# Receiver half of a graph layer's first product: a table of values per node, read through masked hidden values of 128 consecutive edges

## What is computed

```python
r = edge_vec / norm(edge_vec);  sh1 = sqrt(3) * r
xs, xd = x[edge_src], x[edge_dst]
s1 = concat([xs[:, :8], xd[:, :8]])                 # 16 scalars
v1 = concat([xs[:, 8:], xd[:, 8:]]).reshape(E,16,3) # 16 vectors
w  = mlp(emb, fc1_w1, fc1_w2)                       # hidden 16 -> 512 weights per edge
s_t = a1 * (s1 @ Wss + vdot1 @ Wvv)                 # per edge 16 -> 8
v_t = a1 * ((s1 @ Wsv) * sh1 + v1 @ Wvs)
w2 = mlp(emb, fc2_w1, fc2_w2)                       # 384 weights per edge
scal, gates, vecs = second product of s_t, v_t, w2
edge_out = [tanh(scal), vecs * tanh(gates)] * norm
x = layernorm(x + segment_sum(edge_out, edge_dst))
```

## Time and profile before

| | |
|---|---|
| median of 3 runs | 6061.76 us |
| profiled execution, first to last instruction (span) | 6434.2 us |
| PE / DVE busy in it | 5895.3 / 5884.2 us (92% / 91%) |
| POOL / ACT busy in it | 4974.7 / 3993.5 us (77% / 62%) |
| DMA engines, mean busy share | about 0.43 in the loop |
| granted PE clock, mean | 0.983 of 2.4 GHz |

### The profile page before, as it was taken

One profiled execution on the slowest core, in us unless ns is written; L12 is line 12 of the kernel. 1 busy time (PEld: TensorE's weight loads), 2 busy tenths in 40 slices (PEclk: granted clock), 3 DMA queues, 4 the chain that ended last, 5 costly groups with the idle time before them and its releaser, 6 DMA issues. The chain is left out here.

```text
span 6434.2 us, 221220 instructions
## 1 busy us (share of the span) xinstructions
PE 5895.3 (92%) x68616; PEld 5688.0 (88%) x68616; DVE 5884.2 (91%) x7326; ACT 3993.5 (62%) x12507; POOL 4974.7 (77%) x6875
## 2 busy tenths in 40 slices
PE   4999999999999999999999999999999999999997
PEld 3898989889999988988999889889989899999997
DVE  7899999999999998989999989999999899999998
ACT  5666666666666666666666666666666566666663
POOL 6777777777778777877877778777878778787884
PEclk9999999999999999999999999999999999999998
DMA  5444444444444444444444444444444444444442
GB/s 144 89 87 85 88 91 87 86 88 89 87 88 91 86 88 88 89 86 85 92 87 87 87 85 91 86 86 88 92 86 92 85 86 93 86 93 87 92 88 54
DMA packets 1671119, 569.93 MB, mean 89 GB/s; under 512 B 1535146, under 2 KB 1619083, under 8 KB 1670536
## 3 DMA queue, kind: packets, MB, share of 16 engines
q1 hardware_dynamic: 1567911, 516.43, 36.8%
q0 software_dynamic: 103168, 53.03, 6.0%
HBM read 302.19 MB, written 7.26 MB: 48 GB/s over the span
## 5 line engine op out<-in xcount | busy, mean ns | idle before, releaser
L1043 PE MATMUL p<-identity,prods 128*128 128x128 f32 x29016 | 3580.0, 276 | 157.1 <-issue 81.0
L654 POOL DMA_INDIRECT nodes<-x_rows,idx x3224 | 3104.0, 963 | 704.7 <-issue 615.1
L1043 PEld LDWEIGHTS p<-identity,prods 128*128 128x128 f32 x29016 | 3219.4, 143 | 185.0 <-issue 163.6
L1038 PE MATMUL pw<-w_stack,hid_t 128*128 128x128 bf16 x22568 | 1679.3, 220 | 229.6 <-issue 110.8
L1038 PEld LDWEIGHTS pw<-w_stack,hid_t 128*128 128x128 bf16 x22568 | 1435.3, 99 | 316.6 <-issue 138.9
L1292 DVE TENSOR_TENSOR prods<-pw,V 128x2048 f32<-128x2048 f32 x403 | 922.6, 2289 | 177.2 <-remote 83.3
L1337 DVE TENSOR_TENSOR prods<-pw,M 128x1024 f32<-128x1024 f32 x806 | 975.9, 1211 | 15.9 <-issue 6.7
L1347 DVE TENSOR_TENSOR prods<-pw,VT 128x1536 f32<-128x1536 f32 x403 | 704.8, 1749 | 59.7 <-remote 53.2
L870 ACT ACTIVATE off_hot<-node_iota,off_base 128x42 f32<-128x42 f32 x3216 | 747.1, 318 | 0.0
L1314 DVE TENSOR_TENSOR prods<-pw,S 128x1024 f32<-128x1024 f32 x403 | 490.0, 1216 | 84.6 <-PE pw L1038 76.0
L610 POOL TENSOR_TENSOR vr<-V,r 128x384 f32<-128x384 f32 x403 | 347.5, 862 | 244.9 <-issue 185.5
(11 more groups left out here) (136 smaller groups left out, 8242.5 us busy)
## 6 DMA issues: line engine op xcount, KB each, us to landing
dstb<-in_dst SPq DMA_DIRECT2D x403, 504.0 KB
nodes<-x_rows,idx POOLq DMA_INDIRECT x3224
emb_stack<-emb_parts SPq DMA_DIRECT2D x2418, 20.0 KB
emb<-in_emb_t SPq DMA_DIRECT2D x403, 40.0 KB
hid_t<-hid_parts SPq DMA_TRANSPOSE x806
idx<-in_src SPq DMA_DIRECT2D x403, 4.0 KB
xw<-x SPq DMA_DIRECT2D x403, 7.9 KB
vecs<-in_vec SPq DMA_DIRECT2D x403, 12.0 KB
```

The source lines that it names most:

```text
L654: nc.gpsimd.indirect_dma_start(nodes[:, p, t, side, :], None, x_rows, bass.IndirectOffsetOnAxis(ap=idx[:, p, side, t:t + 1], axis=0)).then ...
L1038: mm = nc.tensor.matmul(pw[:, slot, t, :], hid_t[:, layer, a.par, t, :], w2_stack[:, lo:lo + W], start=True, stop=True)
L1043: return nc.tensor.matmul(out, column, identity[:, :], start=first, stop=last, is_transpose=True)
```

## The change

For the receivers the product is turned around. For one node and one hidden unit h, the receiver's features times the part of `fc1_w2` that belongs to h is the same for all edges into that node. So a table is made: per node 16 rows (one per h) of 64 values. The value of an edge is the sum over h of its hidden value times the node's row h.

- `nodes_made` (PE, 2 matmuls of 256 columns, each period) and `nodes_out` (ACT) make 64 nodes of the table in two periods; `store_nodes` (SP, every second period) stores them to `t_rows` in DRAM and loads the features for the next 64. The first 4 groups of 64 are made in the setup.
- `load_near` (SP): for each of the 8 tiles of a block, a register load of the tile's first receiver, then a DMA of 128 rows of 64 f32 values (8 nodes by 16 h) from `t_rows`.
- `hidden_near` (PE, 2 matmuls of 512 columns) makes the hidden values of the first layer transposed, 8 times, one for each of 8 nodes; rows with a large negative bias (`off_rows_of`, loaded by `stack_off`) make the copies of the wrong nodes zero after the ReLU in `near_hidden` (ACT).
- `receivers` (PE): 8 f32 matmuls, K = 128, 64 columns, from masked hidden values and table rows, into PSUM bank `pz`. `node_scalars`, `receiver_dots` and accumulation in `pz` bring the result into the sums.
- The first layer's per-edge weights shrink from 512 to 256 columns (7 fills become 5) and DVE's first-layer products and their transposes to half. `off_rows`, `hot_rows`, `dst_rows_made`, `directions`, the loads of `dstb`, `xw`, `vecs`, inverse lengths and weights in the loop go. `out_sums_back` and `vectors_back` (ACT) go, and DVE's `vectors_made` comes.
- The edges of a tile are now 128 in a row. Receivers, senders, weights and unit vectors of all edges are transposed on PE in the setup, in 7 chunks of 4 x 128 tiles, and kept in SBUF (`r_all`, `w_all`) or stored as `rec`, `base_rows` and `off_rows_of`.
- The flag's conditions change: a tile may span at most 8 nodes, a block 42.

```diff
-L1, L2 = 512, 384
+L1, L2 = 256, 384
-KINDS = 7
+KINDS = 5
...
+            def load_near(a):
+
+                p = a.par
+                sp.wait_ge(near_base_in[p], a.k(16))
+                sp.sem_inc(begun, 1)
+                wait(sp, d_mm, a.before(2).n(1, 1))
+                sp.sem_inc(begun, 1)
+                wait(sp, t_stored, a.before(1).k(16, 16 * (LEAD - 1)))
+                sp.sem_inc(begun, 1)
+                for t in range(G):
+                    first = nc.sync.value_load(near_base[0:1, p, t:t + 1], min_val=0, max_val=N - 1)
+                    sp.dma_start(t_near[:, p, t, :], t_rows[bass.ds(first * H, NEAR * H), :]).then_inc(t_near_in[p], 16)
+
+            def store_nodes(a):
+
+                sp.wait_ge(t_out, a.n(1, 1 + 2 * LEAD))
+                sp.sem_inc(begun, 1)
+                sp.dma_start(t_nodes[bass.ds((a.half + LEAD) * CHUNK, CHUNK), :],
+                             t_stage[0:CHUNK, :, :, :, :].rearrange("n h a j w -> n (h a j w)")).then_inc(t_stored, 16)
+                sp.wait_ge(t_mm, a.n(1, 1 + 2 * LEAD))
+                sp.sem_inc(begun, 1)
+                sp.dma_start(xt[:, 0, :, :], x6[:, :, bass.ds((a.half + (LEAD + 1)) * CHUNK, CHUNK)]).then_inc(xt_in[0], 16)
...
+            def hidden_near(a, half):
...
+                nc.tensor.matmul(near_ps, w1_near[:, :, :].rearrange("k n h -> k (n h)"),
+                                 emb_stack[:, p, 512 * half:512 * half + 512], start=True, stop=True).then_inc(near_mm, 1)
...
+            def receivers(a, before, is_general):
...
+                for t in range(G):
...
+                        mm = nc.tensor.matmul(z[:, :, t, :], hid_near[:, P * t:P * t + P],
+                                              t_near[:, a.par, t, :].rearrange("p (c w) -> p c w", w=C), start=(t == 0), stop=(t == G - 1))
+                mm.then_inc(d_mm, 1)
...
-            def dst_rows_made(a):
...
-            def off_rows(a):
...
-            def hot_rows(a):
```

More of the change, by code:

```diff
@@ L9 @@
 WINDOW = 42
-ROWS = 3 * WINDOW
+NEAR = 8
 C = 8
@@ L1159, in body @@
                     if three is not None:
-                        scalar_sums_turned(three, None if five is None else five.n(windows, windows + more))
+                        scalar_sums_turned(three)
                     if four is not None:
                         out_sums(four)
+                    if two is not None:
+                        receivers(two, three, is_general)
                     if zero is not None:
                         hidden(zero, is_general)
-                    if two is not None:
-                        pe.wait_ge(pv_done, two.n(2, 2))
-                        fill(two, 2, at.par)
@@ L1168, in body @@
-                    if one is not None and not is_general:
-                        dst_rows_made(one)
                     if four is not None:
                         four_sums_turned(four, windows, more)
+                    if three is not None:
+                        if two is not None:
+                            pe.wait_ge(pss_done, two.n(1, 1))
+                        else:
+                            pe.wait_ge(pgf_done, three.n())
+                        fill(three, 2, at.par)
@@ L1180, in body @@
                         else:
[L1181 to L1185 removed]
                             pe.wait_ge(po_done, three.n(2))
[L1187 removed]
+                        fill(three, 3, at.par)
                     if two is not None:
                         scalar_sums(two)
+                    if one is not None and fast:
+                        hidden_near(one, 1)
@@ new lines, in _ @@
+            last = recs[:, NS - 1 - (NCH - 1) * BLOCKS * P // G, G:2 * G].bitcast(F32)
+            wait_kept(dve, NCH - 1, 1)
+            if NS != FULL:
+                done(nc.vector.scalar_tensor_tensor(last, last, 1.0, fresh[:, :], ALU.subtract, ALU.mult))
+                nc.vector.tensor_scalar(last, last, 1.0, None, ALU.add).then_inc(fresh_done, 1)
+            else:
+                nc.vector.sem_inc(fresh_done, 1)
+            first, period, most, least = (bounds[:, k, :] for k in range(4))
@@ new lines, in _ @@
+            over, other = excess[:, 0, :], excess[:, 1, :]
+            done(nc.vector.tensor_tensor(over, first, period, ALU.subtract))
+            done(nc.vector.tensor_tensor(other, over, most, ALU.add))
+            done(nc.vector.tensor_scalar(other, other, 1.0 - WINDOW, None, ALU.add))
+            done(nc.vector.scalar_tensor_tensor(over, over, -1.0, other, ALU.mult, ALU.max))
+            done(nc.vector.scalar_tensor_tensor(over, most, 1.0 - NEAR, over, ALU.add, ALU.max))
+            done(nc.vector.scalar_tensor_tensor(over, least, -1.0, over, ALU.mult, ALU.max))
```

1442 lines of the change are left out of this document (877 added, 565 removed).

## The result

| | before | after |
|---|---|---|
| median, us | 6061.61 (6059.76 to 6062.57) | **9650.29** (9647.01 to 9653.0) |
| ratio | | 1.5917 (95%: 1.5894 to 1.594) |
| span of a clean profiled execution, us | 6065.0 | 9650.3 |
| period of the loop, us | 14.68 | 23.17 |
| PE / DVE busy | 95% / 97% | 64% / 49% |

The kernel is 59% slower. All comparisons from here on are with that one.

What follows compares the result with a forecast made beforehand. SP's DMA-issuing queue was taken as the bound: 14.5 - 3.4 + 12.3 = 23.4 us a period. 240 + 403 x 23.4 + 45 = 9715 us under the profiler, times 0.942, gave 9150 us, range 7700 to 9900.

Steps and rivals of the forecast that it cites:

- SP's queue is the bound, and the change puts eight loads on it: SP's DMA-issuing queue, over 90% full before, goes from 14.5 to 23.4 us a period, far above PE's 12.8.
- 1.23 us a tile: Table load on SP's queue: register load 0.451, bounds check, register operation, DMA 0.331, gaps; eight times makes 9.85 us.
- The other items: SP's queue per period: near_base 0.47, stack_off 0.88, store_nodes 0.66, semaphores 0.44 us added; 3.4 us of old loads gone.
- Eight f32 products, 1.2 to 3.1 us: PE's eight f32 matmuls of `receivers` with 64 columns: between 1.2 and 3.1 us a period, taken as 1.6.
- Setup 240 and tail 45: Outside the loop: 240 us until the loop's first product (84 before, range 160 to 300), and 45 us after it.
- times 0.942: Factor on the whole sum, median 6061.76 over profiled span 6434.2 us, turning 9715 us under the profiler into 9150.
- Without the profiler a period takes 14.7, which is the 14.6 of DVE and PE work: Kernel before, loop: the unprofiled period of 14.7 us equals the 14.6 us that DVE and PE work.
- DVE 11.4, PE 12.8 us a period: Compute work in the changed loop: DVE falls from 14.6 to 11.4 us, PE to 12.8 us (12.4 to 14.3).
- Busy under 60% for PE: Sign expected in the profile after: PE busy under 60% and DVE under 50%, idle time mostly ended by DMAs.
- The queue hides its issues: Rival on SP's queue: durations mostly the profiler's, or loads overlap DMAs; PE-bound at 5570 us, chance 0.12.
- The gaps alone are the profiler's: Rival on SP's queue: 80 gaps of 0.045 us vanish, 19.8 us a period, 7790 us; included in the 0.80.
- PE at its lower clock becomes the bound: Rival on PE: at 1.2 GHz its work doubles at most to 25.6 us a period, 9990 us; chance 0.06.

Runs made afterwards that it cites:

- A: Changed kernel, three runs: one register load per block instead of eight, 7833.3 us; also one DMA for eight tiles, 6520.7; eight registers loaded by one instruction, 7985.5.
- B: Kernel before plus eight register loads and eight DMAs of 128 rows of 64 bytes a period into a tile nobody reads; 9759.6 us.
- before_again: The kernel before, unchanged, profiled a second time; 6066.9 us, span 6065.0 us.
- before_relieved: Kernel before with three DMA issues a period (vectors, inverse lengths, weights) moved from SP's queue to ScalarE; 5891.8 us, ratio 0.9714.
- no_table_loads: Changed kernel with the table rows and their bases loaded only for the first blocks, later receiver values being wrong; 5810.6 us.
- one_register: Changed kernel with one register load per block instead of one per tile, all eight tiles reading the first node's rows; 7833.3 us.
- one_dma: Changed kernel with one register load and one DMA for all eight tiles, same bytes, from the block's first rows; 6520.7 us.
- marks_placed: Changed kernel, table loads on ScalarE's queue in pieces of 2, 2, 3, 1, registers loaded in two instructions, receiver marks by one VectorE operation; 6536.7 us.

## Why the prediction was right, and where not

- *SP's queue is the bound, and the change puts eight loads on it*: right, shown by the waits, by A (taking them off gives the time back in the amount of their rows) and by B (adding them to before gives such a loss alone).
- *1.23 us a tile*: measured 1.136. The bounds check and the issue were right; the register load took 0.268 us, not the 0.451 of the earlier trace rows, and one more register operation (`MOVE`, 0.029) and its gap came on top. Over a period I had 9.85 us, and the rows with the dearer first tile add up to 9.24: 0.6 too much.
- *The other items*: `stack_off` I priced like one of `emb_stack`, 0.88 us with its gaps; its rows, with an issue of 0.325, add up to 0.62. `emb_stack` itself stayed at 0.756. `store_nodes` I had at 0.66 us a period, and it took 0.96; `near_base` 0.56 instead of 0.47; what goes is 3.49 instead of 3.4. The change added 23.17 - 14.68 = 8.5 us, and I had 12.3 - 3.4 = 8.9; the queue's work before was 14.7 instead of 14.5. A period of 23.4 was right within 1%, partly by errors that cancelled.
- *Eight f32 products, 1.2 to 3.1 us*: the upper end was misread. L1092 comes twice a period, so its 0.39 us is the busy time of two (0.275 is the mean duration of one), and eight come to 1.5 to 2.2 us. Measured: 768 us in all, 1.9 a period; I had taken 1.6.
- *Setup 240 and tail 45*: the first of the loop's fills on PE starts at 269.6 us and the last at 9600.0, so 270 and 50. The sum was 35 us short here, and some 90 us too long in the loop.
- *"times 0.942"*: **this is the step that failed.** The unscaled sum, 9715 us, is 0.7% from the measured 9650; the scaled one, 9150, is 5% low. I had taken the difference between a profiled 6434 and a timed 6062 us as the profiler's and as proportional. The difference belonged to that one execution: `before_again`, the same kernel, spans 6065.0 us beside 6066.9 timed, and after spans 9650.3 beside 9652.1 timed for the same execution. There was nothing to scale. The measured time lies in my range only because its upper end took in the unshrunk sum.
- *"Without the profiler a period takes 14.7, which is the 14.6 of DVE and PE work"*: wrong in its reading. In the clean profile DVE works 0.974 x 14.68 = 14.3 us, and `before_relieved` shows that SP's queue held the period up.
- *DVE 11.4, PE 12.8 us a period*: DVE 0.485 x 23.17 = 11.2, right. PE 0.653 x 23.17 = 15.1 at a granted clock of 0.79, and 13.0 at 1.00 in `no_table_loads`.
- *Busy under 60% for PE*: 64%; PE is busy for 6180 us at 0.79, and for 5329 us with the same matmuls at 0.976 (`no_table_loads`). DVE under 50%: 49%.

The rivals. *The queue hides its issues*: no; a tile took 1.14 us, far from 0.6. *The gaps alone are the profiler's*: no; the 4.2 us of gaps in a period are part of the time that was measured, since the span with them is the timed duration to within 2 us. At 7790 us this rival lies 1860 us off. *PE at its lower clock becomes the bound*: half true in its condition. The clock did fall, to 0.79 on the mean, between the two levels of 1.2 and 2.4 GHz, but as a consequence: with the queue shorter it rose to 0.855 (`one_register`), 0.934 (`one_dma`) and 0.976 (`no_table_loads`), and with queue work added to before and PE's work unchanged it fell from 0.995 to 0.858. In the changed kernel PE waited 7.5 us in every period, so the clock cost no time there.

The register load's price was the place where page and row were weighed. The Trainium skill ("DMA: Bandwidth & Descriptors", section "Latency and other measured facts") gives a register load a floor of about 600 ns. The load of one register lies below such a floor in these runs: 0.268 us in a row of eight, 0.462 when it stands alone (`one_register`); eight registers in one instruction took 0.717. The measurement decides, and even the row of before was too high for loads in a row. The Trainium skill (the same page, section "Rules for kernel authors") says that spreading issues over engines only saves issue time, and that many small transfers should be made one. This case agrees with both: `before_relieved` gains 2.9% by nothing but issue time, and `one_dma` 1313 us over `one_register` by joining eight transfers.

## What to carry to other kernels

Make a budget of each DMA-issuing queue as of an engine: durations of all its records plus the gaps between them, per period, against the period. A change that replaces arithmetic by loads at places known only at run time pays for each place some 1.15 us of a queue (0.63 with the registers loaded together, their load included), for 8 KB a piece (B) as for 32 KB (the table); if the queue has no such room, join the loads first, or leave the arithmetic. Before a profiled span is scaled to a timed one, profile the unchanged kernel a second time.

## What I had not expected of the hardware

- A register load from SBUF took 0.46 us alone or as the first of a block's eight, and 0.268 us as one of the seven behind it. One instruction for eight registers took 0.717 us on SP's queue and 0.724 on ScalarE's. That is no price per register: the loads of two and of six registers in `marks_placed` took 0.67 and 1.34 us, for a reason that no run here tells.
- The issue of a DMA hardly depends on how many pieces it has: 0.338 us for 128 pieces, 0.409 for 1024. The same issue of 128 pieces took 0.381 us where eight stand behind each other without register loads between them (`one_register`). Other forms cost other times, for a reason that no run here tells: 0.756 for a copy of `emb_stack` (10 x 8 pieces from SBUF), 0.325 for 8 x 8 pieces from DRAM.
- An issue on ScalarE's queue takes as long as on SP's (0.340 us), and the activation behind it starts only then. In `marks_placed` an idle stretch of ScalarE of 1 to 2 us between hand-overs with PE was no room for issues and a register load together.
